# A decoder kernel without its loading stage: its sparse table is built inside the two attentions that follow

## The chip, the cores and the metric

The kernel runs on one core of a Trainium2 chip, as one program. Its engines work in parallel, each through its own list of instructions in order, and wait for each other by semaphores: TensorE (PE, with its weight loads shown as PEld), VectorE (DVE), ScalarE (ACT), GpSimd (POOL) and SyncE (SP), which mostly issues DMAs. The metric is the device time of one execution in microseconds. A profile is a trace of one such execution.

## The reference

Two decoder layers work on x (8 batches of 128 rows and 256 columns) and a context (8 x 128 x 64). In each, three sub-layers are added to x and normalised:

```
x = layernorm(x + L0_attn(x))        # 16 heads, causal, biases
x = layernorm(x + L0_xattn(x, ctx))  # 32 query heads over 8 key heads of the context, no weights
x = layernorm(x + L0_ffn(x))         # 2 of 8 experts by sparse deltas, below
x = layernorm(x + L1_attn(x))        # rope, causal
x = layernorm(x + L1_xattn(x, ctx))
x = layernorm(x + L1_ffn(x))         # 6 of 32 experts and a shared one
```

What matters here is the first FFN. Its experts differ from one dense matrix W in 2048 entries at places mask_idx of a 256 x 256 matrix:

```
deltas = softmax(expert_atom_weights) @ atoms        # 8 x 2048
weighted = deltas * sigmoid(importance)
rows, cols = mask_idx // 256, mask_idx % 256
vals = rw @ weighted[top_idx]
out = x @ W.T + segment_sum((x[:, cols] * vals).T, rows).T
```

Places can occur twice, and their values add up.

## The kernel before

The program runs in stages, each closed by a barrier of all engines: a loading stage (`load_first`), the four attentions with the first FFN between them (`attention`), routing, experts, and the final sum.

`load_first` loads the arrays and turns the sparse entries into a table in DRAM (`sparse_table`, one row of 8 expert values for each of the 65536 places). VectorE and ScalarE make the softmax of the atoms' weights and the sigmoid of the importance, TensorE multiplies by the atoms (L1066), and VectorE splits the values into three bf16 parts (`f_w`, L1116). Equal places are added up by comparisons: for each of 16 tiles of 128 entries VectorE compares all 2048 places with the tile's own (L1092, into one of four buffers `f_eq`), and TensorE multiplies each comparison with the tile's values (L1073, 16 products). The sum of the parts is `f_sum`. Meanwhile SyncE fills the table with zeros from `f_m_re`.

`attention` is software-pipelined over units: a unit is one batch of one attention, 8 units each for the first attention (a0, units 0 to 7), the cross-attention (x0, 8 to 15), the second attention and the second cross-attention. Between unit 15 and the second attention four places host the first FFN. A host place w has 2 cycles in the first attention and 4 in the others, and in a cycle (w, c) each engine runs, in a fixed written order, its part of several units: scores of a pair of heads of unit w+1, exponentials of a pair of unit w, output of unit w-1, projections of unit w+2. Places -3 to -1 fill the pipeline. In a cycle TensorE first computes scores and transposed scores (L336, L344, L348, with maxima subtracted at L356), then values (L428) and transposes or projections. VectorE takes the maxima of the scores (L730), which free the banks for the next scores, then its share of normalising (L761, L768), residuals and statistics (L778 to L791), and the norm (L797). GpSimd computes the reciprocal deviation by a power (L928), which VectorE's norm waits for, stages the queries of the cross-attention (L918, L919) and issues the scatters of the table's rows, 16 indirect DMAs that each wait for the one before (L936), two in each of the places 0 to 7. SyncE issues the loads of the first 18 units' expert weights at the stage's start and, when all scatters have landed, reads the table back into `f_m_re` (L244). VectorE re-orders it into `f_m` in cycles 1 and 2 of place 15 (L858); the transposed first FFN tile is copied by ScalarE (L618) after that, since it lies in the same memory.

Of the kernel before, what the change touches and what calls it, by code (L numbers as in the profile page):

```python
# [34 lines left out]
EQ = 4  # L35
LOW = 18
# [73 lines left out]
def attention(nc, cfgs, T, F):  # L110
# [46 lines left out]
    with Stage(nc, "at") as stage, ExitStack() as ctx:  # L157
# [39 lines left out]
        table_back = sem("table_back")  # L197
        m_ready = sem("m_ready")
# [14 lines left out]
        PA, PB, M, PV = T.PA, T.PB, T.M, T.PV  # L213
        SB, STB = T.SB, T.STB
# [23 lines left out]
        @block.sync  # L238
        def _(sp):
            sp.wait_ge(T.low_cleared, 1)  # L240
            T.low_count = load_units(T.arrays, T, range(LOW), sp, T.low_loaded)
            sp.wait_ge(placed, NS // 128 * 16)
            for j in range(KT):
                sp.dma_start(F.m_re[:, j, :], F.table[j * 128 * 256:(j + 1) * 128 * 256, :]  # L244
                             .rearrange("(p r) e -> p (r e)", p=128)).then_inc(table_back, 16)


        @block.tensor
        def _(pe):
            def transpose_x(m):  # L250
                if not (has(m) and own[m].project):
                    return
# [43 lines left out]
            def project_v(m):  # L296
                if not (has(m) and projected_v(own[m])):
                    return
                pe.wait_ge(q_ready, m + 1)
                if own[m] is ATTN0:  # L300
# [139 lines left out]
            def transpose_att(m):  # L440
# [3 lines left out]
                if m > 0:  # L444
                    pe.wait_ge(res_done, m)
                for j in range(KT):
# [3 lines left out]
            def project_out(m):  # L450
# [6 lines left out]
                last.then_inc(out_done, 1)  # L457

# [51 lines left out]
            for w, c, count in hosts:  # L510
# [29 lines left out]
                ffn(w, c)  # L540


        @block.scalar
        def _(act):
# [90 lines left out]

            for w, c, count in hosts:
# [20 lines left out]
                else:  # L657
                    copy_maxima(unit(w + 1))
                    copy_xt(unit(w + 3))


        @block.vector
        def _(dve):
# [51 lines left out]
            def value_rows(m):  # L715
                if not has(m) or own[m] is not ATTN0:
                    return
                if m < 3:
                    dve.wait_ge(v_ones, 6)
                dve.wait_ge(vproj_done, m + 1)  # L720
# [49 lines left out]
            def residual(m):  # L770
# [5 lines left out]
                if own[m].out:  # L776
                    if own[m].bias:
                        dve.tensor_tensor(T.xb[:], x, T.b_o[:], ALU.add).then_inc(bias_done, 1)  # L778
# [74 lines left out]
            def ffn(w, c):  # L853
                t = tile_of(w, c)
                if w == FFN_AT - 1 and c in (1, 2):
                    dve.wait_ge(table_back, 16 * KT)
                    j = c - 1
                    dve.tensor_copy(F.m[:, j, :, :], F.m_re[:, j, :].rearrange("p (r e) -> p e r", e=E0)).then_inc(m_ready, 1)  # L858
# [21 lines left out]

            for w, c, count in hosts:
# [18 lines left out]
                ffn(w, c)  # L900

# [5 lines left out]
        def _(pool):  # L907
# [22 lines left out]
            def place_entries(t):  # L930

                if not 0 <= t < NS // 128:
                    return
                if t > 0:
# [3 lines left out]

            for i in range(3):
# [9 lines left out]
            pool.wait_ge(pads_cleared, 2)  # L949
            for w, c, count in hosts:  # L950
# [905 lines left out]
```

## Time and profile before

| | us |
|---|---|
| median of 3 runs | 892.03 |
| lowest, highest | 890.66, 892.32 |
| the profiled execution | 893.14 |
| its span, from first to last instruction | 891.2 |
| first transposes of the attention on TensorE | 40.23 |

Shares of the span that the engines are busy: PE 83%, PEld 51%, DVE 53%, ACT 33%, POOL 23%. A share is an average over stages with different limits, so the stage is read for itself: by its timeline (start, duration, and in brackets how long the engine stood idle before and what ended it) and by windows (busy time of each engine in a stretch, the granted TensorE clock as a share of its full level, the busy share of the DMA engines and the GB/s moved).

### The profile page before, as it was taken

Reading aid. Unit: us, or ns where it says so; the run is one execution under the profiler, and the core shown is the slowest. Engines: PE = TensorE matmul, PEld = TensorE weight load, DVE = VectorE, ACT = ScalarE, POOL = GpSimd, SP = SyncE. Lnnn points to the kernel's source line nnn. Section 1 sums busy time; section 2 is a strip of 40 time slices with the busy share of each in tenths; the row PEclk is TensorE's granted clock in tenths of the full one; section 3 lists DMA queues with packets and bytes.
Section 4 is the critical chain, followed back from the end, with each engine's and each line's share of the span. In section 5 each row is a group of like instructions: output and inputs, shape, how many; then the busy total and the mean of one; then the engine's idle time right before and its main releaser. Section 6 shows DMA issues by size and latency. Waiting matters only on the chain. (4 is left out here: it accounts for less than half of the span.)

```text
span 891.2 us, 18175 instructions
## 1 busy us (share of the span) xinstructions
PE 741.9 (83%) x6832; PEld 457.1 (51%) x6887; DVE 473.9 (53%) x1240; ACT 294.9 (33%) x702; POOL 209.2 (23%) x253
## 2 busy tenths in 40 slices
PE   3589987877799999999999998699699999999900
PEld 3457765555554455655566666467344433434400
DVE  5755565566448886455453454259533333333447
ACT  0013233444420102333333333233265544555400
POOL 3111222010000000000000000054456556665500
PEclk9999999999969999999999999879899999999955
DMA  9493002000000000000000000087122222222273
GB/s 295 122 293 110 2 3 95 1 3 1 2 1 1 0 1 1 1 1 2 2 1 2 1 3 1 1 224 214 32 75 84 78 84 80 82 84 78 73 244 103
DMA packets 48123, 55.28 MB, mean 62 GB/s; under 512 B 7366, under 2 KB 43174, under 8 KB 47334
## 3 DMA queue, kind: packets, MB, share of 16 engines
q1 hardware_dynamic: 38246, 34.11, 13.2%
q0 software_dynamic: 6656, 16.85, 5.6%
q10 hardware_dynamic: 3136, 3.15, 1.1%
q8 instruction: 58, 0.95, 0.5%
q14 instruction: 27, 0.22, 0.1%
HBM read 41.45 MB, written 12.65 MB: 61 GB/s over the span
## 5 line engine op out<-in xcount | busy, mean ns | idle before, releaser
L730 DVE TENSOR_REDUCE nmf<-bank 128x4 f32<-128x512 f32 x192 | 123.7, 686 | 123.6 <-PE bank L336 123.5
L590 ACT ACTIVATE pt<-bank 128x512 f32<-128x512 f32 x192 | 104.2, 595 | 252.8 <-PE bank L356 252.8
L336 PE MATMUL bank<-kk,qT 32*128 32x256 f32 x768 | 109.2, 401 | 15.9 <-ACT pt L590 8.3
L928 POOL TENSOR_TENSOR rstd<-vare,half 128x1 f32<-128x1 f32 x32 | 17.5, 546 | 376.9 <-DVE vare L791 376.9
L336 PEld LDWEIGHTS bank<-kk,qT 32*128 32x128 f32 x768 | 67.2, 184 | 51.2 <-issue 35.3
L1531 PE MATMUL bank<-wgu,g_xgT 128*64 x256 | 90.5, 476 | 2.1 <-ACT g_xgT L1568 1.2
L1531 PE MATMUL bank<-g_wgu,g_xgT 128*64 128x352 f32 x256 | 90.5, 476 | 0.0
L356 PE MATMUL bank<-nm,sel 32*128 32x128 f32 x768 | 84.5, 338 | 0.0
L1496 POOL DMA_INDIRECT out_rows<-g_og,g_out_row x64 | 63.9, 998 | 64.9 <-DVE g_og L1600 54.5
L348 PE MATMUL bank<-qT,kk 32*128 32x512 f32 x256 | 74.6, 659 | 2.0 <-ACT pt L590 1.5
L1551 PE MATMUL bank<-wd,g_hT 128*64 x256 | 68.9, 392 | 0.2
L1551 PE MATMUL bank<-g_wd,g_hT 128*64 128x256 f32 x256 | 69.0, 392 | 0.0
L1491 POOL DMA_INDIRECT g_xg<-x_rows,g_x_row x64 | 62.6, 978 | 23.0 <-issue 18.2
L356 PEld LDWEIGHTS bank<-nm,sel 32*128 32x128 f32 x768 | 57.4, 191 | 18.1 <-issue 18.1
L1600 DVE COPY g_og<-bank 128x256 f32<-128x256 f32 x64 | 27.0, 421 | 65.9 <-remote 52.6
L491 PE MATMUL bank<-f_m,f_xT 128*128 128x512 f32 x128 | 59.6, 605 | 0.6 <-DVE f_acc L837 0.5
L1582 ACT ACTIVATE g_wgu<-wgu 128x704 f32 x64 | 50.7, 792 | 14.5 <-issue 9.1
L428 PE MATMUL bank<-pt,vaug 128*32 128x128 f32 x1024 | 43.0, 287 | 10.3 <-DVE att L768 9.6
L1594 DVE TENSOR_TENSOR g_h<-bank,g_sil 128x176 f32<-128x176 f32 x64 | 21.7, 339 | 55.9 <-ACT g_sil L1572 43.6
L1531 PEld LDWEIGHTS bank<-wgu,g_xgT 128*64 128x64 f32 x256 | 30.1, 137 | 33.2 <-issue 31.3
L1551 PEld LDWEIGHTS bank<-wd,g_hT 128*64 128x64 f32 x256 | 29.8, 136 | 21.7 <-issue 12.5
L1568 ACT ACTIVATE g_xgT<-bank 128x256 f32<-128x256 f32 x64 | 24.1, 377 | 40.0 <-remote 29.4
(242 smaller groups left out, 1346.5 us busy)
## 6 DMA issues: line engine op xcount, KB each, us to landing
wgu<-in_L_ffn_w_gate SPq DMA_DIRECT2D x4, 1408.0 KB
wgu<-in_L_ffn_w_up SPq DMA_DIRECT2D x4, 1408.0 KB
wd<-in_L_ffn_w_down SPq DMA_DIRECT2D x32, 176.0 KB
g_y<-out_rows SPq DMA_DIRECT2D x4, 768.0 KB, 16.7
g_y<-out_rows ACTq DMA_DIRECT2D x4, 768.0 KB, 17.4
sparse_table<-f_m_re SPq DMA_DIRECT2D x2, 1024.0 KB
f_m_re<-sparse_table SPq DMA_DIRECT2D x2, 1024.0 KB, 5.9
f_idx_row<-in_L_ffn_mask_idx SPq DMA_DIRECT2D x1, 1024.0 KB
```

The costliest lines, as they stand in the source:

```text
L336: return pe.matmul(bank, q, k, start=first, stop=r == 1, skip_group_check=True)
L348: pe.matmul(STB[u][:, :], T.kk[v % 3][rows, kind * 128:(kind + 1) * 128], T.qT[v % 3][rows, :], start=not own[v].causal, stop=False, skip_ ...
L356: return pe.matmul(STB[u][:, slot * 128:(slot + 1) * 128], T.sel[rows, which, :], T.nm1[rows, :], start=False, stop=slot == 3, skip_group_ ...
L428: last = pe.matmul(PV[quarter * COL:(quarter + 1) * COL, at * 128:(at + 1) * 128], cfg.stationary(vaug(v), kv), T.pt[2 * (t % 2) + u][:, s ...
L491: last = pe.matmul(expert_bank(t, q)[:, :], F.xT[t % 2][:, j * 128:(j + 1) * 128], F.m[:, j, 2 * q:2 * q + 2, :], start=(j == 0), stop=(j ...
L590: act.activation(T.pt[2 * (t % 2) + u][:, :], STB[u][:, :], ACT.Exp, scale=own[v].scale).then_inc(exp_done, 1)
L730: dve.tensor_reduce(T.nmf[v % 2][:, 2 * (c % 2) + u, at:at + 4], SB[u][:, :].rearrange("p (h k) -> p h k", h=4), AX.X, ALU.max, negate=Tru ...
L1491: pool.indirect_dma_start(G.xg[n % 4][:], None, G.x_rows[:, :], bass.IndirectOffsetOnAxis(ap=G.x_row[:, n:n + 1], axis=0)).then_inc(gather ...
L1496: pool.indirect_dma_start(G.out_rows[:, :], bass.IndirectOffsetOnAxis(ap=G.out_row[:, n:n + 1], axis=0), G.og[n % 4][:], None).then_inc(sc ...
L1531: last = pe.matmul(gu[n % 2][rows, 0:2 * MI], G.xgT[n % 2][:, j * 128:(j + 1) * 128][:, rows], w, start=(j == 0), stop=(j == KT - 1), skip ...
L1551: last = pe.matmul(down_bank[n % 2][rows, 0:D], G.hT[n % 2][:, j * 128:(j + 1) * 128][:, rows], w, start=(j == 0), stop=(j == 1), skip_gro ...
L1582: act.activation(G.wgu[n % 2][:], T.wgu[:, bass.ds(unit, 1), :, :].rearrange("p a k n -> p (a k) n"), ACT.Copy).then_inc(wgu_ready, 1)
```

## The change

The loading stage is gone, with its barrier. Small constant arrays are packed into one. SyncE loads the packed array, one x tile and two weights first, then the other x tiles, then the sparse arrays, zeros for the table and the later weights; ScalarE's queue loads Wv and its bias. The waits for these stand where they are first used. The values of the entries are made between the cycles of the first attention's fill (places -1 to 1), the comparisons and their products, three in a cycle, in places 9 and 10, with the places converted to 16-bit integers first and six buffers instead of four; the scatters, one in a cycle, in places 11 to 14. The expert weights' loads stand behind the scatters and the read-back, and both re-orderings of the table in cycle 3 of place 15. GpSimd clears `f_m_re`, which VectorE did.

```diff
-EQ = 4
+EQ = 6
+        EQUAL_AT, PER = B + 1, 3
+        def cycle(w, c):
+            return 4 * (w - EQUAL_AT) + c
 @block.sync
+            for dst, src in first:
+                sp.dma_start(dst, src).then_inc(first_loaded, 16)
+            for dst, src in third:
+                sp.dma_start(dst, src).then_inc(third_loaded, 16)
+            for dst, src in sparse:
+                sp.dma_start(dst, src).then_inc(sparse_loaded, 16)
+            sp.wait_ge(cleared, 1)
...
             sp.wait_ge(T.low_cleared, 1)
-            T.low_count = load_units(T.arrays, T, range(LOW), sp, T.low_loaded)
-            sp.wait_ge(placed, NS // 128 * 16)
+            sp.wait_ge(placed, ST * 16)
             for j in range(KT):
                 sp.dma_start(F.m_re[:, j, :], F.table[j * 128 * 256:(j + 1) * 128 * 256, :]
                              .rearrange("(p r) e -> p (r e)", p=128)).then_inc(table_back, 16)
+            T.low_count = load_units(T.arrays, T, range(LOW), sp, T.low_loaded)
 @block.tensor
+                else:
+                    pe.wait_ge(first_loaded, 16 * len(first))
+                if m == 1:
+                    pe.wait_ge(third_loaded, 16 * len(third))
...
+                if (w, c) == (-1, 1):
+                    transpose_atoms()
+                if (w, c) == (0, 1):
+                    expert_atoms()
+                for t in range(PER * (cycle(w, c) - 1), PER * cycle(w, c)):
+                    if 0 <= t < ST:
+                        add_equal(t)
 @block.vector
-                if w == FFN_AT - 1 and c in (1, 2):
+                if w == FFN_AT - 1 and c == 3:
                     dve.wait_ge(table_back, 16 * KT)
...
+                dve.tensor_scalar(F.eq[t % EQ][:], F.idx16, F.col_f[:, t:t + 1], None, ALU.is_equal).then_inc(eq_ready, 1)
+            def atom_weights():
+                dve.wait_ge(sparse_loaded, 16 * len(sparse))
+                dve.tensor_reduce(F.eawmax[:], F.eaw[:], AX.X, ALU.max, negate=True).then_inc(v, 1)
+                dve.tensor_copy(F.col_f[:], F.idx_col[:]).then_inc(columns_ready, 1)
+                dve.tensor_copy(F.idx16, F.idx_row[:]).then_inc(columns_ready, 1)
...
+                if (w, c) == (-1, 0):
+                    atom_weights()
+                if (w, c) == (-1, 1):
+                    normal_weights()
+                if (w, c) == (0, 0):
+                    atom_columns()
+                if (w, c) == (1, 0):
+                    entry_values()
+                for t in range(PER * cycle(w, c), PER * cycle(w, c) + PER):
+                    if 0 <= t < ST:
+                        equal_places(t)
+                if cycle(w, c) == 7:
+                    entry_sums()
 @block.gpsimd
+                if t == 0:
+                    pool.wait_ge(v, sparse_done)
+                    pool.wait_ge(zeroed, 16 * KT)
...
             for w, c, count in hosts:
                 if c == 0:
                     stage_qk(unit(w + 3))
-                    place_entries(2 * w)
-                if c == 1:
-                    place_entries(2 * w + 1)
                 if c == count - 1:
                     rstd(unit(w - 1))
+                place_entries(cycle(w, c) - 8)
+def first_loads(a, T):
+    return [(T.packed[:], a["packed"]), (T.x_all[:, 0, :], a["x"][0]),
+            (T.a0_wqk[:, :, 0:256], ktiles(a["L0_attn_Wq"])), (T.a0_wqk[:, :, 256:512], ktiles(a["L0_attn_Wk"]))]
```

`normal_weights`, `atom_columns`, `entry_values`, `entry_sums`, `transpose_atoms`, `expert_atoms` and `add_equal` hold the instructions of the old stage unchanged, with new waits.

On VectorE, in a cycle of the cross-attention (`nmf` are the maxima, `rec`, `att` and `kk` normalised outputs and keys, `f_eq` the comparisons), there stands before:

```order
L730 TENSOR_REDUCE nmf_153<-bank 128x4 x2
L761 RECIPROCAL rec<-bank 128x32
L768 TENSOR_TENSOR att<-bank,rec 128x16x2x8
L699 TENSOR_TENSOR kk_160<-bank,kinds 128x256
```

and in cycle 1 of place 9 and the start of cycle 2 now:

```order
L811 TENSOR_REDUCE nmf_148<-bank 128x4 x2
L842 RECIPROCAL rec<-bank 128x32
L849 TENSOR_TENSOR att<-bank,rec 128x16x2x8
L778 TENSOR_TENSOR kk_155<-bank,packed 128x256
L969 TENSOR_SCALAR f_eq_214<-f_idx_210,f_col_f 128x2048
L969 TENSOR_SCALAR f_eq_215<-f_idx_210,f_col_f 128x2048
L969 TENSOR_SCALAR f_eq_216<-f_idx_210,f_col_f 128x2048
L811 TENSOR_REDUCE nmf_148<-bank 128x4 x2
```

The three comparisons stand ahead of the next cycle's maxima.

On GpSimd, in the first attention and the start of the cross-attention's staging, there stands before:

```order
L948 MEMSET qs_163 128x640
L936 DMA sparse_table<-f_sum_220,f_pos 65536x8 x4
L928 ISA
L928 TENSOR_TENSOR rstd<-vare,half 128x1
L936 DMA sparse_table<-f_sum_220,f_pos 65536x8 x2
```

and in places 11 to 13 of the cross-attention now:

```order
L1100 DMA sparse_table<-f_sum_218,f_pos 65536x8 x3
L1089 TENSOR_TENSOR rstd<-vare,half 128x1
L1100 DMA sparse_table<-f_sum_218,f_pos 65536x8
L1079 COPY qs_158<-x_all 128x16x8 x2
L1080 COPY qs_158<-c_all 128x4x16
L1100 DMA sparse_table<-f_sum_218,f_pos 65536x8 x3
L1089 TENSOR_TENSOR rstd<-vare,half 128x1
L1100 DMA sparse_table<-f_sum_218,f_pos 65536x8 x4
```

Three scatters now stand ahead of each unit's power, four between two powers, where the cross-attention had none before.

## Rows read from the trace of the kernel before

**Rows 1.** Timeline, first stage: start, duration, instruction, idle before and its end

```profile
11.94 6.99 PE L1066 MATMUL bank<-f_eawT,f_atoms 64*128 64x8 f32 x32 [0.25 <-DVE f_eawT L1100]
...
21.48 14.44 DVE L1092 TENSOR_SCALAR f_eq<-f_idx_row,f_col_f 128x2048 bf16<-128x2048 int32 x12 [0.70 <-PE bank L1073]
...
35.98 0.60 PE L1073 MATMUL bank<-f_w,f_eq 128*128 128x24 bf16 x16 [0.59 <-DVE f_eq L1092]
...
40.23 0.66 PE L262 MATMUL bank<-ident,x_all 128*128 128x128 f32 x2 [3.65 <-PEq L107]
```

**Rows 2.** Windows at the start: length, clock, DMA share, GB/s

```profile
1.00:6.00 5.00, 1.00 0.87 251
6.00:11.00 5.00, 1.00 1.03 254
11.00:16.00 5.00, 1.00 1.15 328
16.00:21.00 5.00, 1.00 1.05 400
```

**Rows 3.** Windows of VectorE's small sparse operations: length, busy, clock, DMA

```profile
10.99:11.72 0.73, 0.39 (x2) 1.00 1.10 329
11.73:13.00 1.27, 1.23 (x4) 1.00 1.28 258
19.04:20.80 1.76, 1.56 (x6) 1.00 1.05 442
35.83:37.47 1.64, 1.22 (x7) 1.00 0.00 0
```

**Rows 4.** Timeline of TensorE and VectorE in the first attention's fill

```profile
47.83 0.44 PE L262 MATMUL bank<-ident,x_all 128*128 128x128 f32 x2
...
54.47 0.42 DVE L721 TENSOR_TENSOR vaug_wide<-bank,b_v 128x256 f32<-128x256 f32 x1 [0.52 <-PE bank L302]
...
55.88 1.29 DVE L730 TENSOR_REDUCE nmf<-bank 128x4 f32<-128x512 f32 x2 [0.99 <-PE bank L336]
...
65.14 1.29 DVE L730 TENSOR_REDUCE nmf<-bank 128x4 f32<-128x512 f32 x2 [1.42 <-PE bank L336]
...
75.31 1.29 DVE L730 TENSOR_REDUCE nmf<-bank 128x4 f32<-128x512 f32 x2 [1.20 <-PE bank L336]
```

**Rows 5.** Windows, busy PE, PEld, DVE, ACT, POOL: fill, then cross-attention unit

```profile
64.00:72.00 8.00, 7.80 (x120) 6.25 (x121) 3.62 (x8) 2.71 (x7) 0.97 (x1) 1.00 0.78 230
176.02:188.76 12.74, 9.83 (x158) 7.32 (x158) 7.97 (x19) 5.73 (x12) 1.19 (x4) 1.00 0.01 3
```

**Rows 6.** Timeline of TensorE in that unit, one cycle's start

```profile
180.76 0.48 PE L336 MATMUL bank<-kk,qT 32*128 32x256 f32 x2 [0.74 <-ACT pt L590]
```

**Rows 7.** Groups of VectorE by form: one-source operations, four-byte and two-byte source

```profile
L1092 DVE TENSOR_SCALAR f_eq<-f_idx_row,f_col_f 128x2048 bf16<-128x2048 int32 x16 | 19.2, 1276 | 0.7 <-PE bank L1073 0.7
...
L1410 DVE TENSOR_SCALAR g_slot_hot<-g_slot_is,row 128x384 bf16<-128x384 bf16 x8 | 2.4, 306 | 0.0
```

**Rows 8.** Windows where the granted clock falls

```profile
148.00:150.00 2.00, 0.85 (x7) 0.34 (x4) 1.38 (x3) 0.28 (x1) 0.00 (x0) 1.00 0.99 414
154.00:156.00 2.00, 2.00 (x17) 1.43 (x10) 1.28 (x2) 0.50 (x2) 0.00 (x0) 0.50 0.00 0
```

**Rows 9.** Timeline of GpSimd: a scatter under load, one without

```profile
51.47 0.96 POOL L936 DMA_INDIRECT sparse_table<-f_sum,f_pos  x1 [6.16 <-DMA sparse_table<-f_sum,f_pos]
...
84.09 0.96 POOL L936 DMA_INDIRECT sparse_table<-f_sum,f_pos  x1 [1.90 <-DMA sparse_table<-f_sum,f_pos]
```

**Rows 10.** Timeline at the cross-attention's end; the read-back among the DMA issues

```profile
240.04 0.54 POOL L928 TENSOR_TENSOR rstd<-vare,half 128x1 f32<-128x1 f32 x1 [9.81 <-DVE vare L791]
...
247.68 3.98 DVE L858 COPY f_m<-f_m_re 128x2048 f32<-128x2048 f32 x2
...
257.19 0.39 ACT L618 ACTIVATE f_xT<-bank 128x256 f32<-128x256 f32 x1
...
f_m_re<-sparse_table SPq DMA_DIRECT2D x2, 1024.0 KB, 5.9
```

More of the change, by code:

```diff
@@ L213, in attention @@
         PA, PB, M, PV = T.PA, T.PB, T.M, T.PV
+        ST = NS // 128
+        EQUAL_AT, PER = B + 1, 3
+        first, second, third = first_loads(T.arrays, T), second_loads(T.arrays, T), third_loads(T.arrays, T)
+        sparse = sparse_loads(T.arrays, F)
+        sparse_done = 18
+        def cycle(w, c):
+            return 4 * (w - EQUAL_AT) + c
         SB, STB = T.SB, T.STB
@@ L239, in _ @@
         def _(sp):
+            for dst, src in first:
[5 more added lines that the diff above has]
+            sp.wait_ge(cleared, 1)
+            for j in range(KT):
+                sp.dma_start(F.table[j * 128 * 256:(j + 1) * 128 * 256, :].rearrange("(p r) e -> p (r e)", p=128),
+                             F.m_re[:, j, :]).then_inc(zeroed, 16)
+            later = later_loads(T.arrays, T)
+            for dst, src in later:
+                sp.dma_start(dst, src).then_inc(T.later_loaded, 16)
+            T.later_count = 16 * len(later)
             sp.wait_ge(T.low_cleared, 1)
-            T.low_count = load_units(T.arrays, T, range(LOW), sp, T.low_loaded)
-            sp.wait_ge(placed, NS // 128 * 16)
+            sp.wait_ge(placed, ST * 16)
             for j in range(KT):
@@ L299, in project_v @@
                 pe.wait_ge(q_ready, m + 1)
+                if m == 0:
+                    pe.wait_ge(second_loaded, 16 * len(second))
                 if own[m] is ATTN0:
@@ L457, in project_out, with transpose_atoms, expert_atoms, add_equal @@
                 last.then_inc(out_done, 1)
+            def transpose_atoms():
+                pe.wait_ge(v, 3)
+                pe.transpose(M[0:ATOMS, 384:384 + E0], F.eaw[:], T.ident[0:E0, 0:E0]).then_inc(eaw_on_pe, 1)
+            def expert_atoms():
+                pe.wait_ge(v, 4)
+                for t in range(ST):
+                    last = pe.matmul(M[:, 384 + t * E0:384 + (t + 1) * E0], F.atoms[:, t * 128:(t + 1) * 128], F.eawT[:],
+                                     start=True, stop=True)
+                last.then_inc(eaw_on_pe, 1)
+            def add_equal(t):
+                if t == 0:
+                    pe.wait_ge(v, 12)
+                    pe.wait_ge(res_done, B)
+                pe.wait_ge(eq_ready, t + 1)
+                for u in range(ST):
+                    last = pe.matmul(M[:, u * 24:(u + 1) * 24], F.eq[t % EQ][:, u * 128:(u + 1) * 128],
+                                     F.w3[:, t, :], start=(t == 0 and u == 0), stop=(t == ST - 1), skip_group_check=True)
+                last.then_inc(eq_used, 1)
             def ffn_transpose(t):
@@ L634, in ffn @@
                     ffn_weight(t + 1)
+            for dst, src in second:
+                act.dma_start(dst, src).then_inc(second_loaded, 16)
             for w, c, count in hosts:
```

253 lines of the change are left out of this document (110 added, 143 removed).

## The prediction

> **What bounds the kernel now.** I read the times first, then the timeline of the first 45 us, the DMA rate in stretches of it, the timelines of the first attention's start and of one unit of the cross-attention, and last the rows on scatters and on the end of the cross-attention. The first stage is a serial preface: TensorE multiplies nothing of the decoder before 40.23 us [rows 1]. Inside it VectorE is the engine that everyone waits for: twelve comparisons in a row take 14.44 us [rows 1], while the input arrays move at 251 to 400 GB/s [rows 2] and TensorE needs 0.60 us for each comparison's sixteen products [rows 1]. In the first attention's fill TensorE is busy 7.80 of 8.00 us [rows 5], so whatever it gets there it pays in full. In the cross-attention a unit of four cycles takes 12.74 us, with TensorE busy 9.83 and VectorE 7.97 [rows 5]: neither is full, and TensorE stands idle about 0.74 us of a cycle, waiting for the exponentials [rows 6]. So the change empties a stage where nothing overlaps into two where something does; how much of the 40 us comes back depends on how full these are.
>
> **What goes: the preface.** The first transposes now wait for four loads. In bytes: the packed array 206,848, one x tile 131,072, Wq and Wk 262,144 each, together 0.862 MB; on ScalarE's queue at the same time Wv and its bias, 0.393 MB. At 251 GB/s in 1 to 6 us [rows 2] the sum of 1.255 MB is through at 6.0 us; with 0.3 us until a landing is seen (my allowance) TensorE starts at 6.3. If the four came without sharing it would be 1 + 3.4 + 0.3 = 4.7 us, and with half of the next 1.57 MB mixed in 8.5. Gain 40.23 - 6.3 = 33.9 us (31.7 to 35.5). VectorE's mask and selector copies, moved behind that wait, lie beside the first projection. The other loads: third (1.573 MB) are through at about 12 us by the same rates and are wanted 7.6 us after the first transposes, as in the trace (47.83 - 40.23) [rows 1, 4], at 13.9; the sparse arrays (1.649 MB) at about 16.8, wanted after the second tile's values, 54.47 + 0.42 - 40.23 = 14.7 us after the start [rows 1, 4], at 21.0. Both waits cost nothing while these margins of 2 and 4 us hold. Clearing the table moves from VectorE to GpSimd, which is idle then. SyncE sends the table's zeros and the later weights behind them, and the first expert weights only after all scatters; nobody waits for those before the routing, hundreds of us on.
>
> **What is added to the first attention's fill.** VectorE gets 0.4 us of small operations and the conversion of 2048 places to 16 bits, priced like a comparison of the same shape, 1.28 [rows 7]: 1.65 us, of which 0.99 idle before its next maxima covers a part [rows 4]: 0.7 us. Then TensorE, which before went on with the next scores, waits for the normalised weights: behind both maxima instead of the first (0.5 us) and through a chain that takes 0.73 us in the first stage [rows 3]: 1.2 us. Transposed weights and the sigmoid's rest, 1.23 us [rows 3], fit beneath 1.42 us of idle [rows 4]: nothing. The 16 products with the atoms took 6.99 us in the first stage [rows 1]. That row comes from an engine that had just stood still, and the granted clock has two levels, 1.2 and 2.4 GHz; at the upper one half of it is the lower bound, 3.5. But the trace also shows the clock at 0.50 in 154 to 156 us, after a stretch in which TensorE was busy 0.85 of 2.00 us [rows 8], and these products of 8 columns are thin work too. I take 6.0: the products at the upper level, and a piece of what follows at the lower. The entries' values take 1.76 us against 1.20 of idle [rows 3, 4]: 0.55. Together 0.7 + 1.2 + 6.0 + 0.55 = 8.45 us (5.9 to 11).
>
> **What is added to the cross-attention.** Sixteen comparisons, three in a cycle, twelve in its second unit and four in its third. Their source is now two bytes wide, which no comparison in the trace is at this length: with a four-byte source it took 1.276 us, and a multiplication of the same kind over 384 two-byte elements 0.306 [rows 7]. These are the two ends. Were the short row's time all in its elements, 2048 would take 1.63 us, more than the four-byte row; so a good part of it is fixed, and what the elements cost lies well below. I take 0.75, a little under the middle. Then VectorE becomes the longer engine of that unit: 7.97 + 12 x 0.75 + 0.6 for hand-overs (my allowance) = 17.6 us, 4.9 over 12.74; TensorE has 9.83 + 12 x 0.60 = 17.0 at most and stays beneath. The four in the next unit are 3.0 us, about 1.0 of it in idle time: 2.0. The sums at the end, 1.64 us with their waits [rows 3], delay one set of maxima by about 0.8. Together 7.7 us. At 1.276 a comparison it is 11.2 + 4.1 + 0.8 = 16.1; at 0.306 TensorE's products decide, and with the idle of [rows 6] filled it is about 3.3.
> The Trainium skill has a rule for this in "VectorE: DVE Perf Modes", section "The perf-mode tier table": one-source operations run four times the base rate when source and result are both 16-bit and in SBUF, 693 ns for 2048 elements against 1227 in fp32. No row here shows it at that length; by its figure the 0.75 would be 0.69, an estimate, and the term about 7.0.
>
> **Scatters and the end.** Sixteen scatters, each waiting for the last, move from the first attention, two a unit, to four a unit of the cross-attention. With DMA quiet one cost GpSimd 0.96 + 1.90 = 2.9 us [rows 9]; four are 11.4 to 11.6, and with the 0.54 of the unit's own power (the norm's reciprocal deviation) they fit into 12.74 us, with the copies of x lying in a scatter's flight. The last is issued behind the power at 240.04 (in before's time), is in place near 244, and the table's read-back of 5.9 us [rows 10] ends near 251. The two re-ordering copies of 3.98 us, now one cycle later, would run 251 to 255, and the copy of the first FFN tile that waits for them comes at 257.19 [rows 10]. Cost nothing, with some 2 us to spare; without this cover each us late is a us.
>
> **Sum.** 33.9 - 8.45 - 7.7 = 17.75 us less. The profiled execution took 893.14 us (its span 891.2 and 1.9 around it): 875.4. The median of the runs is 1.1 lower, 892.03, so 874.3; I say 874. With each term at its own ends the cost is 9.2 to 27.1 and the gain 31.7 to 35.5.
>
> **Rivals.**
> *The comparisons stay at the four-byte price.* For it: the scalar is still fp32 and the nearest row is 1.276. Against: a two-byte source shows a short row. Cost 16.1 in place of 7.7: 874.3 + 8.4 = 883.
> *TensorE's clock falls in the cross-attention's loaded unit.* While VectorE compares, TensorE waits more; [rows 8] shows the fall to 0.50 after thin work. For it: idle beside the maxima grows; against: the 48 extra products of each cycle fill part of it. At the lower level the unit's 9.83 at most double: 19.7 + 7.2 = 26.9 against 17.6, and 2 more in the next unit; of these 11 I take 8, since not all of it is bound by the clock: 882. The skill names the rule in "TensorE: Matmul & The Clock Gate", section "Part 1: The HAM clock gate": the throttled state is the default and activity releases it; the trace agrees with both directions.
> *The covers are better than I think.* Products with the atoms at 3.5, comparisons cheap, loads in by 5 us: 2.5 + 4.4 + 1.5 less: 866.
> *Slower: the scatters become the bound.* Under load one cost 0.96 + 6.16 = 7.1 us [rows 9]. Sixteen would be 114 us in four units of 51, GpSimd's power for each norm would queue behind them, and the read-back, the copies and the FFN behind the last: 60 us more, 934. It decides from about 3.0 us a scatter on (12.74 less the power, over four); each us above costs 16, so at 4.1 the gain is gone. For it: 7.1 is in the trace. Against: that was while the expert weights came in, and these now come after the scatters, and the quiet rows are 2.9.
>
> **How the numbers follow.** Forecast (874, its own range 868 to 880) 0.57; comparisons dear 0.17; clock 0.13; better covers 0.08; scatters 0.05. The range that leaves out 2 in 10 at most reaches 865 to 886: it takes in both costly cases and the cheap one. Slower than 0.2% (1.8 us, about what a measurement of this kernel can tell) is the scatters' case, 0.05; within 0.2% needs two costly cases at once, 0.03; faster 0.92.
>
> **What would show it.** TensorE's first transposes between 5 and 8.5 us. A wait of a few us of TensorE before the small transposition and 3.5 to 7 us of products with the atoms in the fill. Comparisons at 0.7 to 0.8 us; at 1.2 the first rival holds. The loaded unit's powers on GpSimd 17 to 18 us apart, the following ones 12.7 again; a granted clock of 0.50 there is the second rival. Scatters 2.9 us apart and no idle of VectorE before the re-ordering copies; if they are 4 us or more apart, the forecast is wrong in the direction of slower. It is wrong as well if TensorE's start is later than 10 us.

## The result and the profile after

The changed kernel takes **883.74 us** (median of 11 runs, 877.96 to 886.55) against 891.99 us for the kernel before, run beside it (11 runs, 889.19 to 899.87). The ratio is 0.9914, with a 95% interval of 0.9886 to 0.9941: about 8 us faster, where 18 were forecast. The profiled execution took 885.41 us with a span of 883.5 us.

The start answers to [rows 1]. These are lines of the changed kernel's timeline (start, duration, engine, instruction, and in brackets the idle time before it with what ended it):

```profile
8.05 7.78 POOL L1115 MEMSET wd<- 64x9216 f32 x1
9.03 6.88 DVE L1022 CAST ident_bf<-packed 128x128 bf16<-128x128 f32 x1 [7.89 <-DMA a_wqk<-in_L_attn_Wk]
9.14 0.66 PE L302 MATMUL bank<-packed,x_all 128*128 128x128 f32 x2 [9.14 <-DMA a_wqk<-in_L_attn_Wk]
...
17.30 0.41 DVE L769 TENSOR_TENSOR qT<-bank,packed 128x256 f32<-128x256 f32 x1
...
17.77 2.07 PE L344 MATMUL bank<-a_wv,xT 128*128 128x256 f32 x4 [3.79 <-DVE qT L769]
```

The same two instructions, and the first queries, in the kernel before:

```profile
0.73 7.77 POOL L1145 MEMSET wd<- 64x9216 f32 x1 [0.29 <-POOLq L1850]
...
37.48 0.22 DVE L1136 CAST ident_bf<-ident 128x128 bf16<-128x128 f32 x1
...
44.79 0.42 DVE L690 TENSOR_TENSOR qT<-bank,b_q 128x256 f32<-128x256 f32 x1 [5.48 <-PE bank L289]
```

TensorE's first transposes moved from 40.23 to 9.14 us. But the first copy on VectorE, 0.22 us long before, now takes 6.88 and ends at 15.91, when GpSimd's clear of part of the expert weights `wd` has ended (8.05 + 7.78 = 15.83). Everything behind it on VectorE waits: the queries come 8.2 us after the transposes, before 4.6 (44.79 - 40.23). TensorE stands idle 3.79 us, and the granted clock falls. The windows (start:end, length, busy time of PE, PEld, DVE, ACT, POOL, granted clock, DMA share, GB/s) show it at the lower of the two levels twice in the fill (first two lines) and once in the cross-attention (last line). The third and fourth lines are the two units of the cross-attention with the comparisons, up to one power each (the norm's reciprocal deviation, on GpSimd), and answer to the second line of [rows 5]; the third begins 0.3 us behind the power before it, at 152.96:

```profile
17.20:30.80 13.60, 12.48 (x42) 7.82 (x42) 5.01 (x13) 0.38 (x1) 0.00 (x0) 0.50 0.98 322
47.90:58.10 10.20, 10.20 (x65) 8.45 (x68) 1.72 (x5) 1.08 (x2) 0.00 (x0) 0.50 0.00 0
153.28:169.28 16.00, 13.91 (x284) 11.22 (x287) 13.55 (x28) 5.73 (x12) 0.88 (x5) 0.89 0.01 3
169.28:185.40 16.12, 13.31 (x280) 10.63 (x272) 12.45 (x27) 5.74 (x12) 2.27 (x5) 1.00 0.01 3
160.50:163.90 3.40, 3.40 (x37) 2.52 (x36) 1.55 (x4) 0.56 (x2) 0.00 (x0) 0.50 0.02 5
```

The wait for the normalised weights, the products with the atoms ([rows 1]: 6.99 us), two scatters and the re-ordering ([rows 9, 10]) read so in the changed kernel's timeline:

```profile
35.51 0.19 PE L505 MATMUL bank<-packed,f_eaw 8*64 8x8 f32 x1 [1.48 <-DVE f_eaw L981]
...
45.15 4.53 PE L510 MATMUL bank<-f_eawT,f_atoms 64*128 64x8 f32 x32
...
230.65 0.96 POOL L1100 DMA_INDIRECT sparse_table<-f_sum,f_pos  x1 [1.90 <-DMA sparse_table<-f_sum,f_pos]
233.52 0.96 POOL L1100 DMA_INDIRECT sparse_table<-f_sum,f_pos  x1 [1.91 <-DMA sparse_table<-f_sum,f_pos]
...
246.71 3.98 DVE L941 COPY f_m<-f_m_re 128x2048 f32<-128x2048 f32 x2 [0.59 <-DMA f_m_re<-sparse_table]
```

And the comparisons among its groups by form (busy us, mean ns; 1276 ns in [rows 7]). Neighbours overlap a little, so sixteen of 747 ns keep VectorE busy for 11.1 us, 0.69 each:

```profile
L969 DVE TENSOR_SCALAR f_eq<-f_idx,f_col_f 128x2048 bf16<-128x2048 uint16 x16 | 11.1, 747 | 0.0
```

To see where the time went, cut the span at five of the powers on GpSimd, which end a unit each. Lengths in us, from the timelines of two profiled executions of each kernel (the second ones are runs of the section below):

| stretch | before | before, again | after | after, again |
|---|---|---|---|---|
| start to TensorE's first transposes | 40.23 | 40.12 | 9.14 | 9.45 |
| to the power of unit 0 (the fill) | 40.16 | 40.24 | 58.10 | 55.17 |
| to that of unit 7 | 85.99 | 85.75 | 85.72 | 86.81 |
| to that of unit 12 (comparisons) | 63.31 | 63.32 | 71.12 | 72.24 |
| to the first FFN tile's | 43.55 | 45.66 | 46.23 | 44.71 |
| to that of unit 31 | 303.85 | 304.05 | 303.80 | 303.86 |
| to the end (routing, experts) | 314.1 | 310.6 | 309.4 | 318.6 |
| span | 891.2 | 889.7 | 883.5 | 890.8 |

31.1 us are gained at the start. The fill gives back 17.9 (14.9 in the second profile) and the comparisons 7.8 (8.9). The fifth line and the last before the span vary between executions of the same kernel by 2 and by up to 9 us, and code that the change doesn't touch runs in the latter.

### The profile page after: what moved, and what is told of

The parts are those of the page before. It is cut to its first block and busy times, and to the rows that moved or that the text cites. A ratio compares the mean times of both kernels' runs of the same rounds, so it can differ in the third digit from the quotient of the medians.

```text
span 883.5 us, 18209 instructions
## 1 busy us (share of the span) xinstructions
PE 757.6 (86%) x6887; PEld 465.5 (53%) x6887; DVE 472.6 (53%) x1240; ACT 301.8 (34%) x702; POOL 212.9 (24%) x254
## 5 line engine op out<-in xcount | busy, mean ns | idle before, releaser
L378 PE MATMUL bank<-kk,qT 32*128 32x256 f32 x768 | 113.0, 412 | 13.1 <-ACT pt L663 5.6
L378 PEld LDWEIGHTS bank<-kk,qT 32*128 32x128 f32 x768 | 69.0, 190 | 49.5 <-issue 34.3
L398 PE MATMUL bank<-nm,sel 32*128 32x128 f32 x768 | 87.2, 346 | 0.0
L390 PE MATMUL bank<-qT,kk 32*128 32x512 f32 x256 | 77.4, 682 | 1.6 <-ACT pt L663 1.1
L1544 POOL DMA_INDIRECT out_rows<-g_og,g_out_row x64 | 63.4, 991 | 58.1 <-DVE g_og L1648 54.5
L398 PEld LDWEIGHTS bank<-nm,sel 32*128 32x128 f32 x768 | 59.3, 197 | 19.5 <-issue 19.5
L1642 DVE TENSOR_TENSOR g_h<-bank,g_sil 128x176 f32<-128x176 f32 x64 | 21.9, 342 | 61.2 <-ACT g_sil L1620 51.4
L470 PE MATMUL bank<-pt,vaug 128*32 128x128 f32 x1024 | 43.8, 291 | 11.8 <-DVE att L849 11.1
L1599 PEld LDWEIGHTS bank<-wd,g_hT 128*64 128x64 f32 x256 | 29.8, 136 | 21.5 <-issue 12.3
L414 PE MATMUL bank<-mask_qk,ident_bf 128*128 128x512 bf16 x128 | 39.9, 391 | 0.3 <-DVE nmf L811 0.2
```

Source lines behind the costliest of these rows:

```text
L378: return pe.matmul(bank, q, k, start=first, stop=r == 1, skip_group_check=True)
L390: pe.matmul(STB[u][:, :], T.kk[v % 3][rows, kind * 128:(kind + 1) * 128], T.qT[v % 3][rows, :], start=not own[v].causal, stop=False, skip_ ...
L398: return pe.matmul(STB[u][:, slot * 128:(slot + 1) * 128], T.sel[rows, which, :], T.nm1[rows, :], start=False, stop=slot == 3, skip_group_ ...
L470: last = pe.matmul(PV[quarter * COL:(quarter + 1) * COL, at * 128:(at + 1) * 128], cfg.stationary(vaug(v), kv), T.pt[2 * (t % 2) + u][:, s ...
L1544: pool.indirect_dma_start(G.out_rows[:, :], bass.IndirectOffsetOnAxis(ap=G.out_row[:, n:n + 1], axis=0), G.og[n % 4][:], None).then_inc(sc ...
L1599: last = pe.matmul(down_bank[n % 2][rows, 0:D], G.hT[n % 2][:, j * 128:(j + 1) * 128][:, rows], w, start=(j == 0), stop=(j == 1), skip_gro ...
```

## The experiments

All of them change the changed kernel, where nothing else is said. The early clears, the later clear and the run without comparisons stand beside a kernel before of 891.3 us, the others beside one of 901.2 to 901.4 us, so between these two groups only ratios (with their 95% intervals) and traces are compared. The theory: **GpSimd's clear holds VectorE's first copies, and with them TensorE and its clock.** The rivals: the copies are slow because of the arriving arrays or as first work; the loss is the products with the atoms; the loss is in the cross-attention.

**Clears before the loads land.** VectorE, idle there, clears the table's staging array and 8 of the 18 units of `wd`.

```
-pool.memset(F.m_re[:], 0.0)
-pool.memset(T.wd[64:128, UNITS - LOW:, :, :], 0.0)
+pool.memset(T.wd[64:128, UNITS - 10:, :, :], 0.0)
+dve.memset(F.m_re[:], 0.0)
+dve.memset(T.wd[64:128, UNITS - LOW:UNITS - 10, :, :], 0.0)
```

> The changed kernel, but every clear is done before the first loads land at 9.0 us: VectorE, which stood still for 7.89 us there, clears the staging array of the table and 8 of the 18 low expert units of wd, GpSimd only the other 10. Theory A (GpSimd's clear of 7.78 us holds VectorE's first copies): the copy of ident_bf takes about 0.2 us in place of 6.88, the first queries stand at 9.1 + 4.6 = 13.7 us in place of 17.3, TensorE's idle of 3.79 us before the first values is gone and the stretch at a granted clock of 0.50 from 17.2 to 30.8 us is shorter or gone; 3.6 us and up to 6.8 more, so 873.5 to 880. Rival B (the copies are slow because the input arrays come in at the same time, or because they are the first work behind a long wait): ident_bf still about 7 us, queries near 17, time 882 to 885 as the changed kernel.

Measured: ratio 0.9855 (0.9814 to 0.9896), 878.67 us. Its timeline:

```profile
9.83 0.23 DVE L1024 CAST ident_bf<-packed 128x128 bf16<-128x128 f32 x1
...
14.39 0.42 DVE L769 TENSOR_TENSOR qT<-bank,packed 128x256 f32<-128x256 f32 x1 [2.72 <-PE bank L329]
...
14.87 1.13 PE L344 MATMUL bank<-a_wv,xT 128*128 128x256 f32 x4 [0.59 <-DVE qT L769]
```

The copy is back at 0.23 us, and VectorE now waits for TensorE and not the other way round. The fill takes 51.25 us in place of 58.10. The interval of the ratio touches that of the changed kernel (0.9886 to 0.9941), so the trace is the better witness. The arrays arrive as before (first transposes at 9.37 us), so the half of rival B that blames them falls; the copy doesn't stand behind a long wait here, and the other half is answered by the next run.

**The same clear, 77 us later**, at the start of the fifth place of the first attention, in one piece.

```
-pool.memset(T.wd[64:128, UNITS - LOW:, :, :], 0.0)   # ahead of the loop
+if (w, c) == (4, 0): pool.memset(T.wd[64:128, UNITS - LOW:, :, :], 0.0)
```

> The changed kernel, but GpSimd's clear of wd (one instruction of 7.78 us) stands at the start of the fifth attention unit, some 50 us later, where no input array arrives and VectorE is in full swing. Theory A: the start is that of the run with early clears (queries near 13.7 us), and in the fifth unit one VectorE operation from SBUF to SBUF grows to several us until the clear ends, the unit is up to 7.8 us longer; time between 876 and 884. Rival B: no operation of VectorE grows there and the units keep their pace; the first copies at the start remain slow, 882 to 885.

Measured: ratio 0.9956 (0.9925 to 0.9987), 886.85 us, more than either theory gave. Its timeline at the start and around the clear:

```profile
9.21 0.23 DVE L1022 CAST ident_bf<-packed 128x128 bf16<-128x128 f32 x1 [8.06 <-DMA a_wqk<-in_L_attn_Wk]
...
84.73 1.29 DVE L811 TENSOR_REDUCE nmf<-bank 128x4 f32<-128x512 f32 x2 [0.45 <-PE bank L378]
84.96 7.77 POOL L1123 MEMSET wd<- 64x9216 f32 x1
86.06 6.71 DVE L822 CAST nm<-nmf 128x16 fp32r<-128x16 f32 x1
...
93.69 2.07 PE L344 MATMUL bank<-a_wv,xT 128*128 128x256 f32 x4 [5.99 <-DVE qT L769]
```

A copy of 16 elements a row takes 6.71 us, until the clear has ended (92.73), with no load on its way; the reduction that reads PSUM, partly beside the clear, takes its usual 1.29. The unit is 19.37 us long, its neighbours 11.87 and 11.88: the clear costs 7.5 us here. At the start it is gone: the first copy takes 0.23 us behind a wait of 8.06 us, so the rest of rival B falls, and the fill takes 51.37 us, counted to unit 0. The 878.67 us of the early clears and these 7.5 make 886.2, so the time is the sum of theory A's own parts, and only its range ended too low.

**The copies on ScalarE**, with the clear unmoved, tells which VectorE work is held.

```
-dve.tensor_copy(T.ident_bf[:], T.ident[:])           # sel and both masks likewise
+act.activation(T.ident_bf[:], T.ident[:], ACT.Copy)  # behind the first copy of transposed x
```

> The changed kernel, its clear of wd unmoved (GpSimd, about 8.05 to 15.8 us), but the four copies that change the type (ident_bf, the two masks, sel) are done by ScalarE, behind its first copy of transposed x. Theory A1 (GpSimd's clear holds only VectorE operations that go from SBUF to SBUF with one source, such as these copies): VectorE's first queries stand at 13.7 us while the clear still runs, TensorE's idle of 3.79 us is gone; time as with the early clears, 875 to 881. Rival A2 (the clear holds VectorE whatever it does): b_k or the queries end only at 15.9 us, time 882 to 886.

Measured: ratio 0.9810 (0.9780 to 0.9841). Its timeline:

```profile
8.04 7.78 POOL L1120 MEMSET wd<- 64x9216 f32 x1
9.29 0.16 DVE L1032 TENSOR_TENSOR b_k<-packed 128x4 f32<-128x4 f32 x1 [8.14 <-DMA a_wqk<-in_L_attn_Wk]
...
14.43 0.42 DVE L779 TENSOR_TENSOR qT<-bank,packed 128x256 f32<-128x256 f32 x1 [4.98 <-PE bank L330]
...
14.91 2.07 PE L345 MATMUL bank<-a_wv,xT 128*128 128x256 f32 x4 [0.59 <-DVE qT L779]
```

With the clear still running until 15.82, VectorE does a multiplication of two SBUF operands (0.16 us) and the queries, one operand from PSUM (0.42 us), unhindered. Of the kinds of work seen beside the clear only the copies from SBUF to SBUF are held: A1 holds, A2 falls. The fill takes 48.38 us, and the interval of the ratio lies below that of the changed kernel beside the same 901 us (0.9860 to 0.9935, last runs of this section).

The Trainium skill states this in "SBUF — State Buffer", section "SBUF: two separate sides": VectorE and GpSimd share a port pair as "an exclusive lock, not a bandwidth split", which a VectorE operation in a two-port mode and a GpSimd operation can't hold together, while a VectorE operation with two SBUF inputs conflicts only with a GpSimd operation that reads SBUF. The three runs agree in each point (6.88 and 6.71 us held, 0.16 not), as far as a clear is one that doesn't read. They show the hold; the ports themselves no row shows.

**Loads in turn**, on top of the copies on ScalarE; the second loads (Wv and its bias) move from ScalarE's queue to SyncE's for it.

```
+sp.wait_ge(first_loaded, 16 * len(first))   # SyncE, ahead of the second and third loads
```

> As the run with the copies on ScalarE, and besides SyncE issues the second and the third loads only when the four first loads have landed. Theory E (the first loads came at 9.0 us in place of the forecast 6.3 because the 1.57 MB of the third loads share the engines with them): first transposes at 5 to 6 us, 3 to 4 us less than the run with the copies alone. Rival F (they are slow by themselves, by the shape of their rows or by start-up): first transposes still at 8 us or later and no gain, or a loss, because x of the other tiles and Wv come later.

Measured: ratio 0.9894 (0.9862 to 0.9926), a loss against the copies alone (0.9810, the intervals lie apart). Its timeline:

```profile
6.18 0.66 PE L306 MATMUL bank<-packed,x_all 128*128 128x128 f32 x2 [6.18 <-DMA a_wqk<-in_L_attn_Wk]
...
17.42 0.41 PE L306 MATMUL bank<-packed,x_all 128*128 128x128 f32 x2 [3.11 <-DMA c_all<-in_ctx]
```

Theory E holds for the start, 6.18 us, though the second loads were held back as well, and which of the two had delayed it isn't told apart. But TensorE then waits 3.11 us for the third loads, and the clock is at 0.50 from 18.0 to 28.3 us. What starts earlier also needs its next arrays earlier.

**The second tile's x ahead of the rest**, on top of that; TensorE waits for the rest only before the third tile.

```
+sp.dma_start(T.x_all[:, 1, :], T.arrays["x"][1]).then_inc(x_loaded, 16)
```

> Copies on ScalarE; loads in turn, but x of the second tile comes alone behind the second loads, and TensorE waits for the rest of the third loads only before the third tile. In the run with loads in turn TensorE started at 6.2 us and then waited 3.11 us, till 17.4, for all of the third loads. If the loads' order was all that spoiled that gain: first transposes at 6.2, second ones at about 14.5, first norm of unit 0 at 54 to 56 us (57.8 with the copies alone), 2 to 4 us less than the run with the copies alone. Rival: the wait only moves on (Wv, the sparse arrays or the table's zeros come later and hold TensorE at the weights' transposition), or the granted clock falls for longer: no gain, unit 0's norm at 58 to 61.

Measured: **ratio 0.9769 (0.9734 to 0.9803), the lowest of this study**, 880.13 us beside 901.37. The second transposes come at 14.24 us without a wait, behind first ones at 6.45, and the power of unit 0 at 56.46. Beside the copies alone (0.9810) the intervals overlap, and of the 3.0 us of lead at the start 1.3 are left at unit 0 (57.78 there) and none at unit 12 (212.80 against 212.77). So that the split gains time is not shown; what is shown is that it takes the 3.11 us of wait away.

**All three:** clears early, copies on ScalarE and loads in turn, without the split.

> Early clears on VectorE and GpSimd, copies on ScalarE and loads in turn together. If theories A1 and E hold: first transposes at 5 to 6 us, queries about 4.6 us later, unless VectorE's own clear of wd (until 9.8 us) holds them, which it can by 0.5 us at most; 3 to 4 us less than with the early clears alone: 874 to 876. If F holds: no less than the run with early clears, 878.

Measured: ratio 0.9852 (0.9818 to 0.9886); first transposes at 6.04, but 2.21 us of wait for the third loads before 16.38, and no gain over the early clears (0.9855). The wait is the one of the loads in turn; whether it alone spoiled the forecast is not shown.

**Without the comparisons** and their 256 products: prices the cross-attention's term.

> The changed kernel without the sixteen comparisons and their 256 products; zeros are scattered in place of the entries' sums (this part of the result is left out). If the term of 7.7 us for the cross-attention is right, its second and third unit take 12.7 us each again (16.3 and 16.1 with the comparisons) and the time falls by 7 to 8 us, to 875.5 to 877. Rival: what is saved there comes back later, because the scatters then start no earlier relative to the end or because the granted clock falls at the end of the cross-attention anyway: less than 3 us, 881 to 884.

Measured: ratio 0.9844 (0.9795 to 0.9893), 877.72 us. The unit behind the first one, in a window from power to power:

```profile
161.56:174.30 12.74, 9.84 (x162) 7.31 (x154) 8.05 (x20) 5.73 (x12) 1.19 (x5) 1.00 0.01 3
```

It is the unit of [rows 5] again to a hundredth of a us (12.74). From unit 7 to 12 it takes 64.07 us in place of 71.12 (72.24 in the second profile): 7.05 to 8.2 us, the price of the comparisons, with the stretch at 0.50 (3.4 us, 6.8 in the second profile) that only the kernel with comparisons has there. By the ratios (0.9914 and 0.9844, the intervals touch) the total is about 6 us lower, nearer to the forecast than to the rival.

**Without the products with the atoms**, and **with these products in the cross-attention** (with the copies on ScalarE).

```
-if (w, c) == (0, 1): expert_atoms()          # left out in the first, on the early clears
+if (w, c) == (EQUAL_AT, 0): expert_atoms()   # the second; entries' values one cycle later
```

> The run with early clears without the sixteen products with the atoms (the entries' values are set to zero, this part of the result is left out). In the run with early clears the first norm of unit 0 came 51.25 us after the first transposes, 11.1 us more than the 40.16 of the kernel before; 6.0 of it was forecast for these products. If that holds: 45 us from the first transposes to that norm, time 872 to 873. Rival G (the rest of the added work, above all TensorE's wait for the normalised weights, makes the clock fall and costs the larger part): 48 us or more and granted clocks of 0.50 between 28 and 49 us as before.

> Copies on ScalarE; the sixteen products with the atoms and the entries' values leave the fill of the first attention and stand in the cross-attention's second unit, one cycle ahead of the first sums. In the run without the products the stretch from the first transposes to unit 0's norm was 42.6 us (51.3 with them), but most of these 8.7 us were lost again by the start of the cross-attention, where the granted clock stayed at 0.50 for 17 us. Theory H (that loss is where the clock happens to fall, not tied to the products): unit 0's norm at 50 to 52 us, 4 to 6 us dearer in the cross-attention, and 0 to 4 us less than the run with the copies alone. Rival I (the fill's thin stretch sets the clock's later fall, so whatever is saved there is lost): a stretch at 0.50 of 10 us or more between 110 and 145 us and no gain, or a loss of 1 to 3 us.

Measured: ratios 0.9797 (0.9750 to 0.9844) and 0.9802 (0.9772 to 0.9831). Windows of the first and of the second:

```profile
122.70:139.70 17.00, 15.10 (x109) 10.45 (x107) 6.28 (x14) 4.87 (x10) 1.19 (x4) 0.50 0.00 1
```

```profile
14.90:124.00 109.10, 95.92 (x1143) 71.99 (x1160) 65.06 (x160) 30.95 (x73) 7.36 (x20) 1.00 0.15 47
141.20:154.90 13.70, 12.56 (x185) 9.64 (x177) 9.60 (x21) 2.77 (x5) 0.00 (x0) 0.50 0.00 1
```

Without the products the fill takes 42.69 us, 8.6 less than the 51.25 with them; moved, 41.75 in place of 48.38, 6.6 less (rival G, 48 or more, falls), and the clock stays at the upper level from 14.9 to 124 us. So they cost 6.6 to 8.6 us there, their part of the clock's fall included. That part goes with them: in each of the nine traces with these products in the fill a stretch of 3.4 to 10.2 us at 0.50 begins while they run or within 0.2 us behind them (47.9 us in the changed kernel), and the three traces without them there show none between 31 and 121 us. Moved, they end at 140.39 us, 0.8 ahead of the last line above, but there a stretch of 6.8 us at 0.50 (from 150.0) comes without them too. But the saving doesn't last: without them the clock stands at 0.50 for 17 us at the start of the cross-attention, and of 8.8 us at unit 0 only 0.9 are left at the first FFN tile (260.75 against 261.67). Moved, they cost 7.0 us in the cross-attention's second unit (21.99 against 15.03), and the FFN begins 0.2 us earlier than with them in the fill. Rival I holds for the balance. Whether the fill's thin stretch causes the clock's later fall, or it falls there by itself, stays open.

**Moved products and split loads together.**

> The two runs before this one together: copies on ScalarE, x of the second tile ahead of the rest, products with the atoms in the cross-attention. If both gains hold: unit 0's norm at 46 to 49 us and a ratio to the kernel before of 0.972 to 0.978, the fastest of all. If the loss at the cross-attention is tied to the earlier fill: no better than the copies alone, 0.98.

Measured: ratio 0.9821 (0.9792 to 0.9851), no better than the copies alone (0.9810) and above the split loads alone, though the intervals touch, with 3.4 and 10.2 us at 0.50 between 141 and 159 us: the gains don't add up.

**Both kernels again,** unchanged.

> The kernel before, unchanged, a second profile of it. In the first profile its expert stage ran at about 3.28 us a slot with VectorE waiting 52.6 us for scatters, the changed kernel's at 3.07 us with 4.6 us of such waits, although the code of that stage is the same; the two profiled executions differ by 7.6 us there and by 0 before it. Theory C (chance of an execution): this profile shows another pace or a mixture, and stretches of 3.07 us. Theory D (the change moves something that the expert stage depends on): 3.28 us and 50 us of waits again.

> The changed kernel, unchanged: how far its start and its end of the cross-attention vary from one execution to the next, and what it gains against the kernel before on the chip on which the other three of this call run. If the clear's hold is the cause of the late start, VectorE's first copy is again held till 15.8 to 15.9 us and the first norm of unit 0 comes at 67 us, give or take 3 us by where the granted clock falls; ratio to the kernel before 0.989 to 0.994. If the hold was an accident of one execution: queries near 14 us and the norm near 60.

Measured: the changed kernel's ratio is 0.9897 (0.9860 to 0.9935) this time, and its first copy is held again, 6.57 us. In the expert stage these are the waits of VectorE for the end of scatters, or where there were none its largest (us in total, times, longest): before, before again, after, after again.

```profile
DVE g_og L1600 <- remote: 52.6, 21, 3.7
```

```profile
DVE g_og L1600 <- issue: 37.3, 54, 1.7
```

```profile
DVE g_og L1648 <- remote: 4.6, 2, 2.4
```

```profile
DVE g_og L1648 <- remote: 50.6, 22, 3.3
```

A slot of the expert stage takes 3.12, 3.00, 3.00 and 3.15 us on the mean in these four. Each kernel shows both paces, so Theory D falls. Whether chance decides from one execution to the next (Theory C) is not shown: the three runs beside the kernel before of 891.3 us and its own second profile all keep to 3.00, and all eight beside the 901 us to 3.12 to 3.17. It is the last line before the span in the table, and the difference of the first two profiles there (4.7 us) need not be the change's.

## Why the prediction was wrong

**The step that failed:** "VectorE's mask and selector copies, moved behind that wait, lie beside the first projection", and with it "Clearing the table moves from VectorE to GpSimd, which is idle then." GpSimd was not idle. Its clear of `wd`, which stood in the first stage at 0.73 us beside a VectorE that only cleared and waited, is pushed behind the table's clear (3.51 us) and the attention's own clears, which came at 40.04 us before (3.8 us), to 8.05 us, just where the copies start. With the table's clear left on VectorE it would by these rows have run from about 4.5 to 12.3 us, an estimate, and still lain across the copies at 9.03. Both steps were priced at nothing, with a cover that looked only at TensorE and at VectorE's own queue. With the hold the fill takes 58.1, 55.2 and 54.4 us (both runs of the changed kernel, the one without comparisons); with the hold gone and the loads not late 51.3, 51.4, 48.4 and 50.0 (early clears, late clear, copies on ScalarE, split loads). The means are 55.9 and 50.3: the hold and the clock's fall behind it cost 5.6 us. By the ratios it is about 5.3 us with the early clears (0.9855 against 0.9914) and 7.8 with the copies on ScalarE (0.9810 against 0.9897). How much of it is the clock's isn't told apart: before 60 us it stands at 0.50 for 13.7 to 23.9 us with the hold and for 3.4 to 13.7 without.

**TensorE's start** was forecast at 6.3 us, with 8.5 as the bound if half of the next loads mix in. It came at 9.14, 2.8 us late, and the sum has three faults. The rate of 251 GB/s is that of the first stage's loads; in the changed kernel, and with the four first loads alone in flight, the same 5 us read so:

```profile
1.00:6.00 5.00, 0.00 (x0) 0.00 (x0) 0.15 (x2) 1.28 (x1) 5.00 (x6) 1.00 0.70 179
1.00:6.00 5.00, 0.00 (x0) 0.00 (x0) 0.15 (x2) 1.02 (x1) 5.00 (x6) 1.00 0.59 172
```

The four loads alone start TensorE at 6.04 to 6.45 us, where the prediction has 4.7 for this case; that they come near its 6.3, a sum for 1.255 MB with Wv and its bias, is luck. The order was wrong too, since the next loads did mix in: at 179 GB/s the 1.255 MB would be there at 8.3 us, an estimate, and not at 9.14. And the bound is mis-summed: by the rates of [rows 2] half of the next 1.57 MB behind 1.255 MB gives 9.4 us and not 8.5, so 9.14 lies inside what the prediction's own rates allow. The other loads were in time, as forecast, for a start at 9 us; for one at 6 us they were not (3.11 us of wait).

**The fill's added work** was forecast at 8.45 us (5.9 to 11). With the hold gone it is 50.3 - 40.2 = 10.1 (8.2 to 11.2), on the dear side: the products with the atoms cost 6.6 to 8.6 against 6.0, the rest (42.69 and 41.75 against 40.2) 1.6 to 2.5 against 2.45. The mechanism was right: the products themselves take 3.73 us where the clock stays up (copies on ScalarE; moved, they take the same), 4.53 here and 6.99 in the first stage, and what follows them runs at the lower level.

**The cross-attention** was right in sum: 7.8 us in the first pair of profiles, 8.9 in the second and 7.05 to 8.2 by leaving the comparisons out, 7.7 forecast. A comparison takes 0.747 us (0.75 forecast), and 0.69 in a row of three. The forecast was a choice between 0.306 and 1.276, so that it fits so closely is luck; 0.69 was the estimate from the Trainium skill's "VectorE: DVE Perf Modes", section "The perf-mode tier table", 8% below the mean of the trace and equal to the pace in a row. VectorE did become the longer engine: in three of the five rows of three the next maxima follow without idle time, as here,

```profile
169.11 2.10 DVE L969 TENSOR_SCALAR f_eq<-f_idx,f_col_f 128x2048 bf16<-128x2048 uint16 x3
171.14 1.27 DVE L811 TENSOR_REDUCE nmf<-bank 128x4 f32<-128x512 f32 x2
```

in the other two they wait 0.31 us for TensorE, and 1.82 in the stretch at 0.50. The cost is otherwise shared out than forecast, 4.0, 3.4 and 0.4 us in three units rather than 4.9, 2.0 and 0.8; the powers are 16.3, 16.1 and 13.1 us apart and not 17 to 18 and then 12.7. Nine of the comparisons end ahead of the first unit's power and seven behind it, not twelve and four. The rival with the four-byte price falls. The rival of the clock is seen, 3.4 us at 0.50, but the unit behind it, at 1.00 throughout, is as long.

**Scatters and end** were right: 2.9 us apart, so the slower rival falls. The re-ordering waits 0.59 us for the read-back, less than the 2 us to spare that were forecast, but the FFN's copy is not late by it: the re-ordering ends at 250.7 us, and ScalarE makes the copy at 254.11, directly behind its exponentials, as before.

By these pieces: 2.8 at the start, 5.6 for the hold and 1.7 in the fill take 10.1 of the 17.75 us of the forecast; 7.7 remain, and 8.3 were measured. The fills of either group vary by 3 to 4 us with where the clock falls, so the agreement is no closer than that. The measured time lies within the stated 865 to 886, but that is luck: the upper end stood there for the two costly rivals, of which one fell and the other shows in 3.4 us only, and not for a hold at the start.

## What to carry to other kernels

When a stage is dissolved, list what every engine did in it, the idle-looking ones too, and look where each long operation lands: a clear that was free beside a waiting engine can hold that engine elsewhere. Long clears on GpSimd belong where VectorE makes no copies within SBUF, or the copies go to ScalarE. An earlier start brings a wait (3.11 us here) unless the second and the third thing wanted are queued in the order in which they are wanted, and even without the wait its lead can be gone 200 us later.

## What the hardware showed that was not expected

- A VectorE copy of 128x16 elements took 6.71 us beside a GpSimd clear, while clears by both engines ran side by side (3.47 us for 128x4096 on VectorE within the 7.77 us clear, in the kernel before).
- GpSimd is longer beside VectorE's comparisons too. The power at 169.28, which starts within the row of comparisons shown above, takes 1.28 us and the one after the last of them 0.55, and so in the second profile of the changed kernel; without comparisons it is 0.54. It costs nothing here, since VectorE's own maxima stand ahead of the norm.

```profile
169.28 1.28 POOL L1089 TENSOR_TENSOR rstd<-vare,half 128x1 f32<-128x1 f32 x1 [15.12 <-DVE vare L874]
185.40 0.55 POOL L1089 TENSOR_TENSOR rstd<-vare,half 128x1 f32<-128x1 f32 x1 [13.85 <-DVE vare L874]
```

- Sixteen products of 8 columns came with a stretch at a granted clock of 0.50 in each of the nine traces that have them in the fill (3.4 to 10.2 us), and none of the three without them has one there.
- The clock column reads 1.00 in the windows at the start of every profile, [rows 2] too, but the first projection runs slower there: its first eight products take 2.08 us at 10.28 in the changed kernel, as at 54.20 at 0.50, and 1.16 at 38.10 at 1.00. By this the 6.99 us of [rows 1] belong to the lower level, as the prediction supposed.
- What is saved in the fill can be lost 80 us later: with the products left out the cross-attention began with 17 us at a granted clock of 0.50, with them 3.4 us.
- The expert stage, with the same code, took 308 to 314 us in the profiles whose kernel before ran at about 891 us, and 317 to 321 where it ran at about 901, with VectorE waiting 34 to 56 us for scatters in the latter (and 52.6 in the first profile of the kernel before).
